# First expert stage reordered by batch, and the head softmax made ready between its last units

## The reference

```python
# stage 5 and 7: eight experts, all of them for every token
def expert_step(acc, w):
    wg, wu, wd = w
    h = jax.nn.silu(x @ wg) * (x @ wu)      # wg, wu: 128 x 512
    return (acc + h @ wd, None)             # wd: 512 x 128
# stage 6: attention whose softmax runs over the 16 heads, not over the keys
dp = jnp.einsum('bhqd,bhkd->bhqk', q, k) * SCALE
attn = jax.nn.softmax(dp, axis=1)
w_avg = jnp.einsum('bhqk,bhkd->bhqd', attn, v)
...
out = w_avg @ w_proj + b_proj
```

## Time and profile before

| | |
|---|---|
| median of 3 runs | 2338.84 us (2335.58 to 2343.15) |
| the profiled execution | 2340.6 us, its span 2338.8 us |
| busy in the span: PE, DVE, ACT, POOL | 1900.2, 1677.2, 1103.4, 995.4 us |
| mean granted TensorE clock | 0.902 of full speed |

### The profile page before, as it was taken

How to read it: one execution, slowest core, us unless ns; L and a number is a source line. 1 busy time by engine, 2 the same in 40 slices (tenths; PEclk the granted TensorE clock), 3 DMA queues, 4 the chain that set the end, 5 groups by cost and what they waited for, 6 DMA issues and landing times.

```text
span 2338.8 us, 32267 instructions
## 1 busy us (share of the span) xinstructions
PE 1900.2 (81%) x12288; PEld 1222.0 (52%) x12288; DVE 1677.2 (72%) x2163; ACT 1103.4 (47%) x1827; POOL 995.4 (43%) x380
## 2 busy tenths in 40 slices
PE   6989899854888876669999587878787777599998
PEld 5444444344444445547777444556455454377776
DVE  4655556155899976456666639998999999566666
ACT  2344445422533212135555336666767676355554
POOL 2476667311377740100000107877787888400000
PEclk8798999976999997769999759989999999699999
DMA  2111111000200000010000000000000000100000
GB/s 69 28 44 41 28 28 29 1 9 11 36 0 1 1 10 5 1 54 14 28 14 1 4 2 1 2 2 1 2 1 2 2 2 2 41 28 24 18 1 19
DMA packets 31567, 35.19 MB, mean 15 GB/s; under 512 B 5619, under 2 KB 19702, under 8 KB 31414
## 3 DMA queue, kind: packets, MB, share of 16 engines
q1 hardware_dynamic: 30886, 32.07, 5.5%
...
q10 hardware_dynamic: 528, 1.05, 0.2%
...
HBM read 17.12 MB, written 1.05 MB: 8 GB/s over the span
## 4 chain that ended last, share of the span: by engine, by line
PE 44%; DVE 17%; issue 16%; POOL 13%; ACT 6%; DMA 2%; SPq 2%; POOLq 0%; DVEq 0%; ACTq 0%; PEldq 0%
PE ps L46 9%; PE ps L47 7%; PE ps L48 7%; POOL AF L642 5%; DVE negm L1972 5%; POOL hc L1193 3%; POOL AF L1193 3%; PE ps L446 2%; PE ps L430 2%; PE ps L1776 2%; PE ps L1799 2%; PE ps L471 2%; PE ps L1767 2%; POOL AF L1725 1%; PE ps L811 1%
## 5 line engine op out<-in xcount | busy, mean ns | idle before, releaser
L1972 DVE TENSOR_REDUCE negm<-ps 128x64 bf16<-128x1024 f32 x256 | 303.5, 1228 | 23.7 <-PE ps L1767 23.5
L1003 DVE TENSOR_TENSOR AF<-ps,AF 128x512 f32<-128x512 f32 x256 | 176.9, 691 | 186.4 <-ACT AF L961 185.9
L642 POOL TENSOR_TENSOR AF<-AF 128x2048 f32<-128x2048 f32 (+3 forms) x73 | 234.2, 3209 | 156.4 <-ACT AF L582 150.4
L46 PE MATMUL ps<-XH,AR 128*128 128x512 f32 x616 | 259.6, 421 | 34.1 <-DVE AF L851 20.0
L1725 POOL TENSOR_TENSOR AF<-AF 128x2048 f32<-128x2048 f32 x64 | 243.8, 3811 | 99.3 <-ACT AF L1883 98.9
L961 ACT ACTIVATE AF<-ps 128x512 f32<-128x512 f32 x256 | 153.0, 598 | 268.7 <-PE ps L48 268.7
L1902 ACT ACTIVATE AF<-ps 128x1024 f32<-128x1024 f32 x192 | 196.9, 1026 | 134.4 <-PE ps L1776 132.4
L47 PE MATMUL ps<-XL,AR 128*128 128x512 f32 x616 | 250.5, 407 | 0.0
L48 PE MATMUL ps<-XH,AR 128*128 128x512 f32 x616 | 249.8, 406 | 0.0
L1767 PE MATMUL ps<-AR 128*128 128x256 f32 x1024 | 215.4, 334 | 16.3 <-ACT AF L1902 11.9
L1776 PE MATMUL ps<-negm,ident_bf 128*128 128x512 bf16 x512 | 160.0, 395 | 82.7 <-DVE negm L1972 82.6
...
## 6 DMA issues: line engine op xcount, KB each, us to landing
...
```

Source lines behind the costliest of these rows:

```text
L46: pe.matmul(out, ah, bh, start=start, stop=False)
L642: pool.tensor_tensor(zacc[u % 2][:, :, c0:512], zacc[u % 2][:, :, c0:512], pt[t % 4][:, :, 0:w], ALU.add).then_inc(s0_zp, 1)
L1003: dve.tensor_tensor(mh[:, m % 3, :], bank(3 + m % 3), msg[:, m % 3, :], ALU.mult).then_inc(m_h, 1)
L1972: dve.tensor_reduce(negm6[:, j % 4, :], bank(2 * (j % 3), 2).rearrange("p (j q i) -> p q j i", j=HJ, i=2), mybir.AxisListType.XY, ALU.max, ...
```

## The change

Stage 5 handles pairs of an expert and a batch instead of experts, in a list `SEQ[0]`: all of batch 0 is done after pair 10 of 16, and experts 5, 0 and 1 are loaded again for batch 1 (11 loads, not 8). From unit 87 on, the output of batch 0 is added to X, its half of the layer norm and its two quarters of XH and XL are made, the 14 first jobs run in units 104 to 117, and the first two scatters in units 120 to 127. The weights of stage 6 are loaded behind the second expert and divided in units 40 to 61. GpSimd's memsets for stage 6 stand behind the second rstd of stage 5. Gate and up products of both expert stages use two banks each in turn. The output of batch 1, its layer norm and its two quarters move into the loop of stage 6; the quarters take the first two places of the projections, all later ones move back one or two places, and the scatters go from the sixth iteration of a group to the eighth. Some tensors of stage 6 get other places in memory. Stage 7 keeps its order.

```diff
+        SEQ = [[(0, 0, 0), (0, 1, 1), (0, 2, 2), (0, 3, 3), (1, 2, 2), (1, 3, 3), (0, 4, 4), (1, 4, 4),
+                (0, 5, 5), (0, 6, 6), (0, 7, 7), (1, 6, 6), (1, 7, 7), (1, 5, 8), (1, 0, 9), (1, 1, 10)],
+               [(b, e, e) for e in range(NE) for b in range(B)]]
...
+        SPLIT_AT = [{PAIR * (LAST_PAIR[k][l - 2] + 1 if l > 1 else 0) + 2: l for l in range(1, N_LOADS[k])}
+                    for k in range(2)]
...
+                if s == 5 and l == 1:
+                    s6_load(q)
...
-                wait(pe, m_h, m - 2)
-                wh, wl = moe_weights(NE * k + e)
+                wait(pe, m_h, m - 1)
+                wh, wl = mwh[l % 2], mwl[l % 2]
                 for g in range(2):
                     o = 512 * g + P * c
-                    ins = mm3(pe, bank(3 * g + m % 3), (wh[:, o:o + P], wl[:, o:o + P]), xt(512 * i, 512))
+                    ins = mm3(pe, bank(2 * g + m % 2), (wh[:, o:o + P], wl[:, o:o + P]), xt(512 * i, 512))
...
+                if s == 5:
+                    s6_ready_pe(pe, n)
...
+        FIRST = kv_jobs(0) + q_jobs(0)
+        SPACED = ([("x", i) for i in (2, 3)] + q_jobs(1) + kv_jobs(1) + q_jobs(2))
+        PLACED = [(job, LB * ((n + 1) // 3) + 2 * ((n + 1) % 3) + 2) for n, job in enumerate(SPACED)]
+        PLACED += [(job, LB * (9 + n // 3) + 2 * (n % 3) + 2) for n, job in enumerate(q_jobs(3))]
...
-        SCATTER_AT = {LB * (g - 2) + 5: g for g in range(2, NB)}
+        SCATTER_AT = {LB * (g - 2) + 7: g for g in range(2, NB)}
...
+        OUT_N = {87: 0, 91: 1}
+        TR_N = {100: 0, 101: 1}
+        JOB_N = {104 + j: JOBS[j] for j in range(len(FIRST))}
+
+        def s6_ready_pe(pe, n):
+            if n in OUT_N:
+                moe_out_pe(pe, 0, OUT_N[n], bank(4 + OUT_N[n]))
+            if n in TR_N:
+                ln_quarter_pe(pe, 6, TR_N[n], bank(4 + TR_N[n]))
+            if n in JOB_N:
...
+                make(pe, *JOB_N[n])
...
+            if n >= PER - 2 * HS:
+                p = n - (PER - 2 * HS)
+                scatter_part(act, link, p // HS, p % HS)
...
+        def s6_ready_pool(pool, link, s):
+            pool.wait_ge(x_done, X_AFTER[s])
             pool.memset(f32(b6), 0.0).then_inc(s6_z, 1)
             pool.memset(f32(bv6), 0.0).then_inc(s6_z, 1)
             pool.memset(f32(ones6), 1.0).then_inc(s6_z, 1)
+            pool.memset(wp6, 0.0).then_inc(s6_z, 1)
+            for q in q6[:2]:
+                pool.memset(f32(q), 0.0).then_inc(s6_z, 1)
+            ln_half_rstd(pool, link, 6, 0)
...
                     if m - 1 in JOBS_AT:
-                        take(*JOBS_AT[m - 1], m - 1)
+                        take(act, *JOBS_AT[m - 1], m - 1)
                     if m in SCATTER_AT:
-                        scatter(SCATTER_AT[m])
+                        for i in range(HS):
+                            scatter_part(act, link, SCATTER_AT[m], i)
...
             for j in range(2 * NTI):
                 maxima(j)
+                if j < 2:
+                    moe_out_dve(dve, 0, 2 + j, bank(6 + j))
+                if j == 2:
+                    dve.wait_ge(x_done, X_AFTER[s])
+                    ln_tiles_stats(dve, link, range(HB, NB))
+                if j == 4:
+                    ln_half_aggr(dve, link, 1)
+                if j == 7:
+                    ln_tiles_norm(dve, s, range(HB, HB + 4))
+                if j == 9:
+                    ln_tiles_norm(dve, s, range(HB + 4, NB))
                 if j % 2 and j >= 3:
                     denominators(j // 2 - 1)
...
+                    if m - 1 in LN_AT:
+                        ln_quarter_dve(dve, s, LN_AT[m - 1], spare_bank(m - 1))
```

More of the change, by code:

```diff
@@ L86, in build @@
         lnt = sb("lnt", [P, 2, 512])
-        AF = sb("AF", [P, AF_WORDS])
         hc = sb("hc", [P, 2, L])
@@ L890, in moe_load @@
             q.wait_ge(x_done, X_AFTER[s])
-            for e in range(NE):
-                n = NE * k + e
+            for l in range(N_LOADS[k]):
+                n = LOAD0[k] + l
+                e = EXPERT_OF[k][l]
                 wait(q, m_wl, n - 1)
@@ L960, in moe_act @@
                 wait(act, m_h, m - 2)
[L961 removed]
+                act.activation(msg[:, m % 3, :], bank(m % 2), ACT.Silu).then_inc(m_sg, 1)
                 if n:
                     hi(act, m - 1)
[L964 to L965 removed]
+                if n in SPLIT_AT[k]:
+                    split(SPLIT_AT[k][n])
+                if s == 5:
+                    s6_ready_act(act, link, n)
             hi(act, PER * k + PER - 1)
@@ L1007, in moe_dve @@
                     total(n // FE - 1)
-                if n % (NT * FE) == 3 and n // (NT * FE) + 1 < NE:
-                    split(NE * k + n // (NT * FE) + 1)
+                if n - 1 in SPLIT_AT[k]:
+                    split(SPLIT_AT[k][n - 1])
+                if s == 5:
+                    s6_ready_dve(dve, link, n)
             finish(PER - 1)
             total(NE * NT - 1)
-            for i in range(NT):
-                dve.wait_ge(m_tr, NT * k + i + 1)
-                xs = X[:, 4 * i:4 * i + 4, :].rearrange("p t d -> p (t d)")
-                dve.tensor_tensor(xs, xs, bank(i % 2), ALU.add).then_inc(x_done, 1)
-            dve.wait_ge(x_done, X_AFTER[s + 1])
+            if s == 7:
+                for i in range(NT):
+                    moe_out_dve(dve, k, i, bank(i % 2))
+                dve.wait_ge(x_done, X_AFTER[s + 1])
         E2, NS, DT, KW = 256, 16, 64, 4
@@ L1709, in s6_load, with make @@
                             a["L1_attn_b_w_proj"].rearrange("(x i d) c -> i d x c", x=SS, i=HS)[i]).then_inc(s6_wp, 16)
-        def s6_clear(pool):
-            pool.wait_ge(x_done, X_AFTER[6])
+        def make(pe, n, job, at):
+            wait(pe, s6_st, n - 1 if at is None else n)
+            if at is not None:
+                pe.wait_ge(x_done, X_AFTER[6] + at // LB)
+            o = job_bank(n, at)
+            if job[0] == "v":
+                _, b, i = job
+                pe.wait_ge(ln_lo, 4 * 6 + 2 * b + i + 1)
+                for t in range(4):
+                    oo = o[:, P * t:P * t + P]
+                    mm3(pe, oo, xt(L * b + 512 * i + P * t, P), (wv_h, wv_l), stop=False)
+                    ins = pe.matmul(oo, ones6[0:64, 0:P], bv6[0:64], start=False, stop=True)
+            else:
+                w, t0 = (SS + job[2], L * job[1] + 512 * job[3]) if job[0] == "k" else (job[2], 512 * job[1])
+                pe.wait_ge(ln_lo, 4 * 6 + t0 // 512 + 1)
+                mm3(pe, o, (rep_h[:, w, :], rep_l[:, w, :]), xt(t0, 512), stop=False)
+                ins = pe.matmul(o, b6[0:64, P * w:P * w + P], ones6[0:64, :], start=False, stop=True)
+            ins.then_inc(s6_pr, 1)
@@ new lines, in take, with stack @@
+        def take(act, n, job, at):
+            act.wait_ge(s6_pr, n + 1)
+            o = job_bank(n, at)
+            if job[0] == "v":
+                act.activation(v6[:, LB * job[1] + 4 * job[2]:LB * job[1] + 4 * job[2] + 4, :].rearrange(
+                    "p t d -> p (t d)"), o, ACT.Copy).then_inc(s6_hi, 1)
+                return
+            wait(act, s6_st, n - 1)
+            act.activation(hi6[:, n % 2, :].bitcast(F32R), o, ACT.Copy).then_inc(s6_hi, 1)
+        def stack(dve, n, job, at):
+            dve.wait_ge(s6_hi, n + 1)
+            o = job_bank(n, at)
+            if job[0] == "v":
+                wait(dve, s6_st, n)
+                dve.sem_inc(s6_st, 1)
+            elif job[0] == "k":
+                _, b, x, i = job
+                dve.scalar_tensor_tensor(out=k6[b][:, x, 512 * i:512 * i + 512],
+                                         in0=hi6[:, n % 2, :], scalar=lo_k, in1=o,
+                                         op0=ALU.mult, op1=ALU.add).then_inc(s6_st, 1)
+            else:
+                _, c, x = job
+                wait(dve, s6_sc, 4 * (c - 1))
+                dve.scalar_tensor_tensor(out=qs6[c % 2][:, x, :], in0=hi6[:, n % 2, :], scalar=lo_q, in1=o,
+                                         op0=ALU.mult, op1=ALU.add).then_inc(s6_st, 1)
@@ L1813, in s6_pe @@
             pe.wait_ge(s6_wp, 16 * HS)
+            pe.wait_ge(m_h, PER)
             scores(0)
             scores(1)
+            for i in (2, 3):
+                moe_out_pe(pe, 0, i, bank(4 + i))
             for j in range(2 * NTI):
@@ L1871, in s6_act @@
-            for n, job, at in FIRST_JOBS:
-                take(n, job, at)
-            act.wait_ge(s6_z, 6)
-            scatter(0)
-            scatter(1)
             def invert(m):
@@ L1966, in s6_dve @@
-            for n, job, at in FIRST_JOBS:
-                stack(n, job, at)
             def maxima(j):
```

381 lines of the change are left out of this document (221 added, 160 removed).

## The result

The changed kernel takes 2325.68 us (median of 13 runs, 2321.50 to 2335.86); the kernel before took 2337.81 beside it. The ratio is 0.9949, with a 95% interval of 0.9937 to 0.9961: faster by 12.1 us. The forecast was 2321, 17.9 us under the 2338.84 of the first three runs; 12.1 came. The profiled execution took 2321.5 us, the quickest of the 13, with a span of 2319.8. Two launches of this study, one of the kernel before (5724.6 us) and one of e3 (4520.4 us), fell into a slow state and count in no ratio.

What follows compares the result with a forecast made beforehand. TensorE was taken to bound stage 5, VectorE stage 6's loop, and no engine the seam between. -77.7 + 27.3 + 6.5 + 2.0 + 24.0 = -17.9 us gave 2321; range 2310 to 2332, with rivals 2301 to 2335.

Steps and rivals of the forecast that it cites:

- Saved at the seam, 77.7: Between stage 5's last `down` and stage 6's first maxima: 78.6 us shrink to 0.9, saving 77.7 us.
- Stage 5, +27.3: TensorE-bound stage 5: moved projections 19.7, transposes 3.6, weight splits 1.0, crowded units 1.5 and memsets 1.5 add 27.3 us.
- the order with three splits more: Stage 5: three more weight splits (11 loads for 8) make waits that add 1.0 us.
- the clears: Start of stage 5: GpSimd's memsets hold VectorE's norms, adding 1.5 us, between 0 and 3.7.
- VectorE's own work, +6.5: Stage 6 loop: 7.0 us of moved adds, statistics, norms and differences, partly in gaps, add 6.5 us.
- Norms against products, +2: Stage 6 loop, j = 7 and 9: norms wait for GpSimd products, adding 2 us, between 0 and 7.6.
- Where the scatters go, +24.0: Stage 6: scatters behind the flush delay VectorE; plain groups 9.6, take groups 12.0, an eighth such group 2.4: 24.0 us.
- 1.4 us more: Stage 6 groups with a take: the late scatter brings the score step at 1496.05 instead of 1494.67; six make 8.4 us.
- The scatter hides: Rival, stage 6: exponentials catch up, the 24.0 falls to about 4, giving 2301 us; chance 0.14.
- Norms and clears blocked throughout: Rival: one norm held behind each long GpSimd instruction, 5.6 + 2.2 us more, giving 2329 us; chance 0.12.
- TensorE slows after each hold: Rival, stage 6: one iteration at the lower clock in each of 14 groups, 31 us more, 2352 us; chance 0.12.
- The change doesn't take the seam away: Rival: some piece of stage 5 is late, a quarter of the 78 us stays, about 2341 us; chance 0.03.

Runs made afterwards that it cites:

- e3: Kernel before with the change's pair order, 11 loads for 8 and two-bank rotation, no work moved: 2336.6 us, ratio 0.9998.
- e4: Kernel before with two banks each for gate and up instead of three in both expert stages: 2335.8 us, ratio 0.9992.
- e5: Changed kernel with GpSimd's clears held back until stage 5's sixteen norms are done: 2327.2 us, ratio 0.9944.
- e1: Changed kernel with every scatter but that of g = 8 back at iteration 5 of its group: 2309.8 us, ratio 0.9886.
- e2: Kernel before with its scatters moved from iteration 5 to iteration 7, nothing else: 2360.5 us, ratio 1.0101.
- e8: Changed kernel with scatters back at iteration 5 (all but g = 8), clears behind stage 5's norms, loop's norms at iteration 4: 2304.9 us, ratio 0.9855.
- e9: Kernel with e8's edits, plus g = 8's scatter at iteration 57 for 55 and exponential tiles moved up 8 bytes: 2296.8 us, ratio 0.9819.

## Why the prediction was right, and where its terms were off

The time came 4.7 us above the forecast of 2321; the sign and the likeliest case held, and the scatter table did cost, as said. In the profiles the stretches from the norms of stage 5 on save 14.2 us for 17.9. That the sum is this close is in part luck: inside stage 5 and inside the scatter term errors of about 3 us and more in opposite directions cancel.

- **Saved at the seam, 77.7.** Measured 77.9, by what the profile before showed. It wasn't certain, though: e4 shows that the seam can take 70 us by the clock alone.
- **Stage 5, +27.3.** Measured 28.4. Inside it: the order with three splits more +2.8 (e3) for 1.0, the clears 2.1 (e5) for 1.5, the rotation 0 (e4) as forecast. A unit with a q or k job took 3.34 us for 3.3 (1309.56 to 1312.90 on TensorE). The v jobs were to run at full clock, 4.9 us a unit; that held in seven profiles (5.0), but in this one TensorE fell to the lower level there, and the way from the first v job to the loop took 44.3 us for 42.7: 1.6 us that I had at nothing. The rest, jobs, transposes and crowded units, is 28.4 - 2.8 - 2.1 - 1.6 = 21.9, where I had 19.7 + 3.6 + 1.5 = 24.8.
- **VectorE's own work, +6.5.** Measured 7.8: the loop's +34.6 less the waits (22.4 with the output add's) and the hold (4.4). VectorE's busy time in the loop says the same, 601.2 for 589.0 us, 12.2 with the hold.
- **Norms against products, +2.** Measured 4.4 in the profiled execution, within my 0 to 7.6. It is a matter of phase, 4.4 or 0.1 to 0.4.
- **Where the scatters go, +24.0.** Measured 22.4 (waits on the maxima +21.8, on the output add +0.6); that the term exists is shown by e1 and e2 from both sides. The parts were off in opposite directions. The plain groups bear the mechanism out: their first waits are 9.7 us for 9.6. The 3.3 us behind them, 13.0 in all, are TensorE at the lower level after its stand, a cost that the term leaves out. Groups with a take wait 11.1 us more than before, the eighth group among them, where I had 14.4; the start of the loop and the v jobs wait 2.4 less. The step that failed is "1.4 us more" for each group with a take. It was worked out from the group of the earlier trace rows with its 1.26 us, but four of the seven stood 1.86 or 1.87 us at the same place, and with the late scatter the first wait is 1.97 to 2.02 in the first five such groups: 0.1 us more than those four, not 1.4. The scatter's share in these groups is 3.8 us by e1, 6.0 by e8, for 9.2, and at g = 8 2.5 (e9) for 2.8.
- **The rivals.** *The scatter hides* is refuted by e1 and e2. *Norms and clears blocked throughout* came half true: every hold is that mechanism, but short clears cost little (0.7 us) and well placed norms escape it. *TensorE slows after each hold*: true in part. The loop's clock went from 0.96 to 0.92, and behind 11 of the 14 stands a few steps run at the lower level, not a whole iteration. The second and third waits are there where that happens and not elsewhere, and they went from 4.3 us to 11.5: 7.2 us of the 21.8 are this rival's mechanism, where it had 31. No run took the clock alone. *The change doesn't take the seam away* is refuted by its 0.60 us.
